# The first block of a count product: pieces loaded while weights are used up, seven products in front of the flips, the first clique rows split early

## The reference, cut to what matters

```
h   = relu(layernorm(x))                     # after layer 0
agg = segment_sum(h[src], dst)               # layer 1
agg = agg / maximum(deg, 1)
...
gathered = x_clique[clique_idx]              # layer 2: clique_idx = dst, node_idx = src, index clamped to 3124
summed   = segment_sum(gathered, node_idx)   # (dst rows beyond the last clique all take the last row)
mean     = summed / maximum(count, 1)
```

## Time and profile before

| | |
|---|---|
| median of 3 runs | 2258.65 us (2257.88 to 2259.93) |
| profiled execution | 2261.03 us, of which the span is 2259.4 us |
| PE busy | 1973.0 us, 87% of the span |
| DVE, ACT busy | 1539.0 us (68%), 1214.8 us (54%) |
| chain that ended last | 80% on PE |
| counting | about 134 to 1160 us |
| end of counting and first product block | about 1160 to 1217 us |
| the thirteen blocks with flips | 1185 to 1535 us |

### The profile page before, as it was taken

How to read it: one execution, slowest core, us unless ns; L and a number is a source line. 1 busy time by engine, 2 the same in 40 slices (tenths; PEclk the granted TensorE clock), 3 DMA queues, 4 the chain that set the end, 5 groups by cost and what they waited for, 6 DMA issues and landing times.

```text
span 2259.4 us, 62757 instructions
## 1 busy us (share of the span) xinstructions
PE 1973.0 (87%) x22348; PEld 1782.8 (79%) x22393; DVE 1539.0 (68%) x3176; ACT 1214.8 (54%) x3140; POOL 136.4 (6%) x120
## 2 busy tenths in 40 slices
PE   1159999999999999999989999999986239999886
PEld 1159999999999999999987777778885228888643
DVE  8588888888888888888866666678845850000254
ACT  5756666666666666666637888889854200000232
POOL 5600000000000000000000000000012410000010
PEclk7579999999999999999999999999998569999987
DMA  8402212222222222221233334447831459888412
GB/s 228 135 32 98 96 73 96 96 80 89 96 86 83 96 93 76 96 99 70 97 135 129 124 125 137 145 144 252 318 116 46 121 175 341 300 301 300 144 54 65
DMA packets 184477, 304.09 MB, mean 135 GB/s; under 512 B 12641, under 2 KB 135958, under 8 KB 184174
## 3 DMA queue, kind: packets, MB, share of 16 engines
q1 hardware_dynamic: 180506, 290.74, 37.1%
q0 software_dynamic: 3904, 12.50, 1.9%
HBM read 202.70 MB, written 100.48 MB: 134 GB/s over the span
## 4 chain that ended last, share of the span: by engine, by line
PE 80%; DVE 6%; ACT 4%; issue 3%; DMA 3%; DVEq 2%; POOL 1%; ACTq 0%; SPq 0%; POOLq 0%
PE ps L826 24%; PE ps L926 23%; PE ps L815 10%; PE ps L809 6%; PE ps L910 6%; PE ps L896 3%; PE ps L1058 2%; PE ps L968 2%; DMA hs<-node_rows 1%; DVE hT_s L1519 1%; POOL edge_area L652 1%; ACT edge_area L1194 1%; PE ps L959 1%; PE ps L976 1%; ACT edge_area L1147 1%
## 5 line engine op out<-in xcount | busy, mean ns | idle before, releaser
L1194 ACT CAST edge_area<-ps 128x392 f16<-128x392 f32 x784 | 405.3, 517 | 393.8 <-PE ps L809 393.8
L826 PE MATMUL ps<-big,rows_area 128*128 128x128 f32 x4802 | 576.9, 277 | 0.0
L826 PEld LDWEIGHTS ps<-big,rows_area 128*128 128x128 f32 x4802 | 551.9, 192 | 0.0
L815 PE MATMUL ps<-edge_area 128*128 128x98 f16 x6272 | 416.2, 208 | 0.0
L1200 ACT COPY big<-ps 128x392 f32<-128x392 f32 x784 | 414.4, 529 | 0.4 <-PE ps L815 0.3
L1665 DVE TENSOR_TENSOR edge_area<-lo_pair,carry 128x1024 f16<-128x1024 f16 x392 | 269.4, 687 | 129.5 <-PE ps L815 126.0
L815 PEld LDWEIGHTS ps<-edge_area 128*128 128x128 f16 x6272 | 330.9, 97 | 0.0
L809 PE MATMUL ps<-edge_area 128*128 128x98 f16 x3136 | 275.6, 209 | 19.2 <-DVE edge_area L1671 11.7
L926 PE MATMUL ps<-big,rows_area 128*128 128x256 f16 (+1 forms) x2450 | 264.7, 272 | 25.7 <-DMA big<-edge_counts 25.7
L926 PEld LDWEIGHTS ps<-big,rows_area 128*128 128x128 f16 x2450 | 236.8, 98 | 53.6 <-DMA big<-edge_counts 25.9
L926 PE MATMUL ps<-big,agg 128*128 128x256 f16 (+1 forms) x2450 | 279.0, 271 | 0.0
(11 more groups left out here) (248 smaller groups left out, 1828.5 us busy)
## 6 DMA issues: line engine op xcount, KB each, us to landing
big<-edge_counts SPq DMA_DIRECT2D x336, 448.0 KB, 4.8
edge_counts<-edge_area SPq DMA_DIRECT2D x49, 1568.0 KB, 5.6
hs<-node_rows POOLq DMA_DIRECT2D x14, 448.0 KB, 4.2
edge_area<-x_stream SPq DMA_DIRECT2D x14, 448.0 KB, 3.9
node_rows<-rows_area SPq DMA_DIRECT2D x1, 3136.0 KB, 13.3
agg_s<-node_rows SPq DMA_DIRECT2D x49, 64.0 KB, 4.9
agg_s<-in_x SPq DMA_DIRECT2D x49, 64.0 KB, 1.8
x_stream<-agg_s SPq DMA_DIRECT2D x49, 64.0 KB, 1.5
```

Of the source, the lines that this page charges most:

```text
L815: last = mm(pair_of(p_weight[s % 4], c), sources_of(slot, r, c), cells_of(oh, slot, r, c), start=(c == 0 and oh is oh_whi), stop=(c == 3 a ...
L826: last = mm(p_sum, h0[:, n, :], w32[:, par, n, :], start=(n == 0), stop=(n == NB - 1))
L1194: nc.scalar.copy(store_slot[:, par, :, cols], p_count[s % 2]).then_inc(sem("count_taken"), 1)
```

## The change

It touches five places.

1. SP: the first clique rows are loaded at the very start of the counting stage (they get a new home behind the planes in `agg`; one of the two clique planes moves into `hT_s`). Block 0's pieces 0 to 3 are loaded behind the store of row tile 45, pieces 4 and 5 behind that of tile 46, piece 6 when the last weigh has ended; each waits until `weigh` has used up the tiles that lie there (`piece_used`, raised by every seventh weigh matmul of the last half).
2. PE, end of counting: the 75 reach matmuls stand in front of `lin1(NB-1)`, and write other PSUM banks.
3. PE, block 0: all seven products first (each waits for its own planes only), then flip and mix by turns. The `piece_used` credit that lets SP load block 1 is raised between the waits of the sixth product. Pieces of block 0 count as used during the mixes, the last in the first mix of block 1. Blocks 1 and 2 are written out in front of the loop.
4. ACT, block 0: sums four pieces, then copies flips 0, 1, 2 before the sums of pieces 4, 5, 6, then copies the rest.
5. DVE: `split_cliques(0)` stands in the counting stage; in block 0 DVE does all seven piece sums, and after the fourth the split for block 1, and only then the six `add_mix`.

```diff
+                load_cliques(0, True)
                 store_half(0, 0, 0)
...
                 store_h(NB - 4, 1)
+                for k in range(4):
+                    sp.wait_ge(sem("piece_used"), k + 1)
+                    load_piece(0, 0, k)
                 store_x(NB - 2, 1)
                 load_x_row(NB - 1, 0)
                 store_h(NB - 3, 0)
-
+                for k in range(4, SUBS - 1):
+                    sp.wait_ge(sem("piece_used"), k + 1)
+                    load_piece(0, 0, k)
+                sp.wait_ge(sem("weighed"), NHALF + 2)
+                load_piece(0, 0, SUBS - 1)
                 sp.wait_ge(sem("half_saved0"), 16 * (NHALF // 2 + 1) + 16)
                 sp.wait_ge(sem("half_saved1"), 16 * (NHALF // 2) + 16)
-                sp.wait_ge(sem("agg_done"), 1)
-                load_cliques(0, True)
-                for k in range(SUBS):
-                    load_piece(0, 0, k)
                 store_h(NB - 2, 1)
...
                     last = mm(p_sum, h0[:, n, :], w32[:, par, n, :], start=(n == 0), stop=(n == NB - 1))
+                    if final and n % SHS == SHS - 1 and n < NB - 1:
+                        last.then_inc(sem("piece_used"), 1)
...
                 row_T(NB - 1, 0)
-                pe.wait_ge(sem("count_taken"), NHALF * SGS + 2)
                 pe.wait_ge(sem("bad_known"), 2)
-                lin1(NB - 1, 0)
                 for j in range(3):
...
                 last.then_inc(sem("bad_summed"), 1)
+                lin1(NB - 1, 0)
+                pe.wait_ge(sem("count_taken"), NHALF * SGS + 2)
...
+                def multiply_first():
+                    pe.wait_ge(sem("taken"), 1)
+                    for k in range(SUBS):
+                        pe.sem_inc(sem("passed"), 1)
+                        pe.wait_ge(sem(f"piece0_{k}"), piece_count(1, 0, 0))
+                        if k == SUBS - 2:
+                            pe.sem_inc(sem("piece_used"), PIECE_CREDIT - (SUBS - 1))
+                        else:
+                            pe.sem_inc(sem("passed"), 1)
+                        pe.wait_ge(sem("planes_ready1"), (k + 1) * SHS)
+                        products(0, k)
+                    for k in range(SUBS):
+                        flip(k, k, 0, 2)
+                        if k:
+                            mix(k - 1, (k - 1) % 2, 0, 0, 2, used=True)
...
+                def count_first():
+                    act.wait_ge(sem("part_added"), 1)
+                    for k in range(SUBS):
+                        if k == SUBS - 3:
...
+                            act.wait_ge(sem("xc_split"), 2)
+                        if k >= SUBS - 3:
+                            copy_flip(k - (SUBS - 3), 0, (k - (SUBS - 3)) % 2, 0)
+                            copy_flip(k - (SUBS - 3), 1, (k - (SUBS - 3)) % 2, 0)
+                        act.wait_ge(sem(f"piece0_{k}"), piece_count(1, 0, 0))
...
+                    for k in range(3, SUBS):
+                        copy_flip(k, 0, k % 2, 0)
+                        copy_flip(k, 1, k % 2, 0)
...
                 weigh_onehots(NDUO - 1, RING - 1)
+                split_cliques(0, 0)
                 row_rest(NB - 5, 0)
...
-                            if cliques and not (first and k == 0):
-                                add_mix(b * SUBS + k - 1, (k + SUBS - 1) % SUBS, first)
+                            if cliques and not first:
+                                add_mix(b * SUBS + k - 1, (k + SUBS - 1) % SUBS)
                             if split and k == SPLIT_AT:
                                 split_cliques(b + 1, 1 - par)
+                        if first:
+                            for k in range(SUBS - 1):
+                                add_mix(k, k, True)
```

More of the change, by code:

```diff
@@ L175, in build_gnn @@
         unused = take(SHS * TD // 2, F16).rearrange("p (j q d) -> p j q d", q=NSUB, d=SUBD)
[L176 to L179, removed]
+        xc_odd = take(2 * 2 * D // 2, F16)
+        xc_in = agg[:, NPAD:NPAD + 2 * D]
+        xc_top, xc_inv = (agg[:, NPAD + 2 * D + n * 2:NPAD + 2 * D + n * 2 + 2] for n in range(2))
+        xc_unit = agg[:, NPAD + 2 * D + 4:NPAD + 2 * D + 8].rearrange("p (s c) -> p s c", s=2)
         flipped = take(4 * W // 2, BF16).rearrange("p (s c n) -> p s c n", s=2, c=2)
@@ L909, in mix, with products @@
                             for l in range(2):
-                                last = mm(p_mix[:, lo:hi], xc_plane[:, par, c, l, :], flipped[:, odd, c, lo:hi],
+                                last = mm(p_mix[:, lo:hi], xc_plane[par][:, c, l, :], flipped[:, odd, c, lo:hi],
                                           start=(c == 0 and l == 0), stop=(c == parts - 1 and l == 1))
+                        if used and lo == 0:
+                            last.then_inc(sem("piece_used"), 1)
                     last.then_inc(sem("mixed"), 1)
+                def products(par, k, width=NSUB):
+                    for j in range(SHS):
+                        sh = k * SHS + j
+                        for p in range(2):
+                            last = mm(p_block[par][:, 0:width, :], planes1[:, sh, p, :] if l == 1 else planes[:, p, sh, :],
+                                      piece[:, par, k, 0:width, j, :],
+                                      start=(sh == 0 and p == 0), stop=(sh == NB - 1 and p == 1))
+                    return last
+                def multiply_first():
[13 more added lines that the diff above has]
+                            mix(k - 1, (k - 1) % 2, 0, 0, 2, used=True)
                 def multiply_block(b, par, i, cliques, first=False, width=NSUB, parts=2):
@@ L922, in multiply_block @@
                             flip(n, k, par, parts)
[L923 to L929, removed]
-                        if cliques and not (first and k == 0):
+                        products(par, k, width).then_inc(sem("piece_used"), 1)
+                        if cliques:
                             if k == 0:
-                                mix(n - 1, (par + 1) % 2, b - 1, 1 - par, 2)
+                                mix(n - 1, (par + 1) % 2, b - 1, 1 - par, 2, used=first)
                             else:
@@ L1868, in count_sorted @@
                     last = V.tensor_copy(reach[:, j, :], p_reach[j])
-                last.then_inc(sem("taken"), 2)
+                last.then_inc(sem("flip_copied"), 2)
                 dve.drain()
@@ L1877, in count_sorted @@
                 dve.wait_ge(sem("agg_done"), 1)
[L1879 to L1892, removed]
-                    V.tensor_scalar(xc_plane[:, par, c, 0, :], rows[:, c, :], xc_inv[:, c:c + 1], None, ALU.mult)
-                dve.drain()
-                for c in range(2):
-                    last = V.scalar_tensor_tensor(out=xc_plane[:, par, c, 1, :], in0=rows[:, c, :], scalar=xc_inv[:, c:c + 1],
-                                                  in1=xc_plane[:, par, c, 0, :], op0=ALU.mult, op1=ALU.subtract)
-                last.then_inc(sem("xc_split"), 1)
             def multiply(l):
```

64 lines of the change are left out of this document (49 added, 15 removed).

## The result

The changed kernel takes **2265.29 us** (median of 7 runs, 2264.07 to 2266.59), the kernel before on the same chip 2257.88 us (7 runs, 2254.62 to 2262.56). The ratio is 1.0032, with a 95% interval of 1.002 to 1.0043: slower by 7.4 us. The forecast was slower, at 2267.4 us.

A forecast was written before the change was run, and what follows sets the result against it. The prediction took PE alone to bound the product, 3.82 us a piece. It added +7.7 us at the end of block 0's sixth mix and +1.0 of echo, +8.7 in all, to the median 2258.65: 2267.4 us, range 2260.0 to 2270.5.

The forecast's parts named there:

- the point: End of block 0's sixth mix, where both kernels are compared: 1217.11 us before, 1224.8 forecast, +7.7 us.
- Pieces earlier, and PE's jump: Before block 0: pieces land before 1180 at no cost; PE's jump falls from 5.86 to 3.3 us, first product 1182.0.
- Reach in front of lin1: End of counting: PE ends 0.8 us earlier, but DVE's chain for tile 48 starts 3.5 us later, at 1178.75.
- Seven products: Block 0 on PE: seven products of 1.53 us plus 1.8 us for a cold start, done at 1194.5.
- DVE's jump: DVE's entry into block 0: a jump of 3.3 us, entering at 1189.9 (1191.1 with the 4.52 of before).
- The new wait: PE's credit at the sixth product starts SP's block 1 pieces at 1191.4; clique rows behind them land at 1203.9.
- DVE's work behind it: After block 1's rows land: split 2.4 us, three sums 3.5, first copy 1.09, done at 1210.9.
- PE's hole and the clock: Before mix 1 PE stands from 1200.7 to 1211.0; mix 1 then runs at 1.2 GHz, 3.0 instead of 1.51 us.
- Mix and add by turns: Block 0 after mix 1: mix and add alternate on one `p_mix`, 2.70 us a round, four times.
- The echo: Block 2's clique rows slip by 1.6 us against PE, because block 0's sums come later: +1.0 us (0 to 1.4).
- A: Rival: block 1's clique rows land about 2 us after issue (1196.4); +3.2 us, or +1.7 with mix 1 warm; chance 0.10.
- B: Rival: block 1's clique rows land in time for DVE; -2.0 us, with the echo -1.0; chance 0.08 without its extreme.

The follow-up runs named there:

- e1: Changed kernel, with DVE's split of block 1's clique rows moved behind the third add in block 0: 2271.15 us, ratio 0.9989 to the kernel before.
- e6: e5 with `lin1(48)` back in front of the reach matmuls: 2267.33 us, ratio 0.9968 to the kernel before.
- e7: e6 with block 0's pieces loaded late, behind the last weigh as in the kernel before: 2271.34 us, ratio 0.9987 to the kernel before.
- e2: Changed kernel with `lin1(48)` back in front of the reach matmuls: 2280.53 us, ratio 1.0029 to the kernel before.
- the third experiment: e3: changed kernel with each block's clique rows loaded in front of its pieces; 2273.19 us, ratio 0.9998 to the kernel before.
- e3: Changed kernel with each block's clique rows loaded in front of its seven pieces: 2273.19 us, ratio 0.9998 to the kernel before.
- e5: e4 with each block's clique rows loaded in front of its pieces: 2269.38 us, ratio 0.9977 to the kernel before.
- e4: Changed kernel with block 0 in its old order on PE, ACT and DVE, and an earlier piece credit: 2269.11 us, ratio 0.998 to the kernel before.
- e8: Changed kernel with an extra 1 MB DRAM copy issued in front of block 1's clique rows: ratio 1.0059, +13.2 us against the kernel before.

## Why the prediction was right

The sign and the place were right: the adds queued behind a wait for a load that is itself queued behind seven pieces. The sum at the point was +7.7 us and +6.5 came out. One mechanism in between, the credit that was to hold SP back, did not act. The sign didn't hang on it: the rows landed 28.1 us after `row_T(48)`, even earlier than the 29.3 us of before, and the loss came from DVE's order, as e1 shows. That +7.7 came so near is in part luck, since misses of both signs met in it. By its own steps:

- **Pieces earlier, and PE's jump.** Taken 3.3 us, from a jump of DVE; it was 2.50 us, and PE's first product came 0.9 us earlier than said. That the load on the queues sets the jump's length had been argued from three unlike jumps; the pair e6 and e7 shows that it lengthens it. (The working also takes 0.115 us for a weigh matmul. The 50 records are 25 matmuls of two each, so one takes 0.23. Nothing waits on that.)
- **Reach in front of lin1.** DVE's bias for tile 48 was said for 1178.75 and came at 1178.42. Right. This delay, and not the credit, set the start of SP's pieces, 16.88 us after `row_T(48)` for 16.30 before.
- **Seven products.** Said to end at 1194.5, ended at 1193.24 after 12.4 us; the length (12.5) was right.
- **DVE's jump.** 3.3 us said, 1.38 measured. A clear miss that changed nothing, since DVE then only waited longer for the rows.
- **The new wait.** The rows were said to be there 30.4 us after `row_T(48)` and DVE's split started at 28.21, so said 2.2 us too late: 1.0 from SP's first piece (at 1190.14, not 1191.4), and 1.2 from a landing in 6.3 instead of 7.5 us behind the pieces. The landing was mis-sized, its mechanism right. The step in front of it was wrong: the credit was said to come when PE reaches the sixth product and to set SP's start. SP didn't wait for it here, its pieces followed the reciprocal loads, and in e2, where SP did wait for it, it came some 1.4 us before the sixth product began.
- **DVE's work behind it.** 7.1 us said, 7.22 measured.
- **PE's hole and the clock.** From 1200.7 to 1211.0 said, 1199.70 to 1208.69 measured. The mix behind it took 3.17 us for 3.0 said. Windows of the hole (columns as above) show the granted clock fall from 1.00 to 0.50, the 1.2 GHz level, with PE idle:

```profile
1200.00:1202.00 2.00, 0.00 (x0) 0.00 (x0) 0.45 (x2) 1.84 (x4) 0.00 (x0) 1.00 0.32 105
1202.00:1204.00 2.00, 0.00 (x0) 0.00 (x0) 1.32 (x7) 1.52 (x7) 0.00 (x0) 0.60 0.01 4
1208.00:1210.00 2.00, 1.31 (x4) 0.49 (x5) 0.63 (x1) 0.00 (x0) 0.00 (x0) 0.50 0.00 0
```

- **Mix and add by turns.** 2.70 us a round said, 2.87 measured. The 1.51 of the earlier trace rows is the time from the start of a mix to the start of the matmuls behind it, which overlap its end. DVE waits for that end, 1.69 us after the start; with the add (1.10) and two hand-overs (0.02 and 0.05) that is 2.87. Four rounds: 0.7 us.
- **The echo.** +1.0 said, none came. Block 0's sums came 0.7 us later after the last mix than before (2.34 us instead of 1.65), not 1.6, and SP's seven issues took 5.43 us instead of 6.20, which made that up. Block 2's clique rows were issued at 1232.82 and landed 6.2 us later, at 1239.0, and DVE came to them at 1239.69.

The misses are -2.2 for the landing, +0.1 for DVE, +0.2 for the slow mix and +0.7 for the rounds: -1.2, which is 7.7 to 6.5. With the echo the forecast for the kernel was +8.7, and the medians say +7.4; 0.9 us of that isn't found at the point, and lies within the interval of the medians. Of the rivals, A needed a landing two microseconds after the issue and got 6.3. B, rows that land in time, is what the third experiment built, and it gave -0.6 instead of -2.0: DVE and PE's second mix were 1.8 us earlier than B says, and then the slow clock took 2.3 us, and a mix of 1.69 us and rounds of 2.87 took 0.9 more than B's.

## What to carry to other kernels

An engine's list is a queue: before a wait is put into it, look at who needs the instructions behind it, and ask of the load it waits for what stands in front of that load in its own queue. Here three adds behind such a wait cost 1.6 us and six adds 9.9. When a change has several parts, price them apart: two of these (the early pieces, 4.3 us of it, and the early first split), with the clique rows loaded first, were worth -9.4 us at the point and -7.4 in time, and the other parts turned that into a loss. And when the undoing of one part changes nothing, look whether a second limit stands right behind it before calling the part harmless.

## What the runs showed of the hardware that I had not expected

- The jump of an engine to new code takes longer while the DMA queues are full: PE 2.46 to 2.92 us with nearly idle queues and 5.77 to 5.86 with seven pieces queued; DVE 1.31 to 1.43 and 3.39 to 4.52. But the earlier trace rows has 3.32 us for a jump of DVE with no data moved, so the load is not all that sets it.
- Neither a hole's length nor what PE did in front of it tells whether TensorE's clock falls. In e2 it fell to 0.50 behind 75 reach matmuls and a hole of 2.90 us; in e6 it stayed at 1.00 behind the same matmuls and one of 2.92 us. e1 and e3, on one chip, have the same list on PE up to there: in e1 it fell after a hole of 2.46 us, in e3 it stayed after one of 2.88 us. Later in e3 it fell in a hole of 2.38 us, behind flips that had waited for ACT. At PE's start the fall came up to 1.3 us after PE had begun to work again. A fall cost 1.5 us (the mix behind the hole of the changed kernel) to 2.3 us (e3) of slow work.
- A 128 KB load took 2.7 to 4.2 us to land when it was issued in front of seven 448 KB pieces (twelve such loads each in the product of e3, e5, e6 and e7), and 6.2 to 8.0 us behind them (twelve each before, in the changed kernel, e1, e2 and e4). With 1 MB more in front it took 10.4 (e8).
